# Hand-ordered instruction lists for a two-layer conditional block: new first and last lists, the condition joined to self outside TensorE, q/k halves spread over three engines

## The chip, the cores and the metric

One core of one Trainium2 chip. The metric is the device time of one launch in microseconds (us). The engines are TensorE (PE, with its weight loads PEld), VectorE (DVE), ScalarE (ACT) and GpSimd (POOL); SyncE (SP) issues every DMA of this kernel.

## The reference, cut to what matters

Eight batches of 256 tokens and 256 features go through two layers, in float32. Layer 0 is a graph attention, layer 1 a transformer block whose norms are set by a condition vector of the batch.

```
# layer 0, F = 256, 16 heads, 20 keys
q_exp = where(v.sum(-1) == 0, 0, q[:, None, :])          # the condition, dropped for all-zero rows
self_feat = concat([v, q_exp]) @ W_self.T + b_self
for d in range(2):                                       # two directions of the adjacency
    cond = A_d.sum(-1); vb = A_d @ w_bias + b_bias
    aff = where(cond > 0, qh @ kh / 4, NEG) + vb         # qh, kh from self_feat
    output += (softmax(aff) @ kv) @ Wout_d + bout_d
x = v + relu(output)
# layer 1, 16 heads of 16, S = 256
nx = ada_rmsnorm(x, cond, ...)
q, k, v = nx @ wq + bq, nx @ wk + bk, nx @ wv + bv       # q and k rotated (rope)
x = x + softmax(q @ k / 4) @ v @ wo + bo
nx = ada_rmsnorm(x, cond, ...)
x = x + (gelu(nx @ w_gate) * (nx @ w_up)) @ w_down       # 1024 hidden
```

## The kernel before

**Numbers in two halves.** The large products run on operands split in a rounded high half and the rest, the low half. `product` (L1076 on) makes three matmuls of each: high by high, high by low, low by high. So each activation and each weight passes two steps: a high half (a copy that rounds), and a low half (whole minus high). For weights these are `whigh` on ACT and `wlow` on POOL or DVE, one per piece of 512 columns, 19 pieces; pieces are loaded by DMA into 11 slots, and a slot is loaded again only once `wlow` of its first piece is done. Six of the slots lie in the tile `ya`, which also holds the condition's weights, the rotated q/k (`t1`, `t2`), their halves and the exponentials.

**Stages of one batch.** Layer 0: x^T is loaded; `xh`, `xl` split it; `rsum` multiplies it by ones, for each token's row sum; `nz` (L789) makes of it 1 or 0, times a one-hot column of the batch; `selfm` (L1134) makes the self product, and its last matmul (L1145) adds the condition: `qz`, which holds the high and low parts of the condition's product for all batches, by `nzT`. `selfc` (ACT, L528) adds the bias and writes `self32`; `selfh` (DVE, L820) and `selfl` (POOL) split it. `kv0`, `kT`, `q0` give keys, values and queries; `affm` the affinities in two halves c; then for each half `am` (DVE, mask), `aadd` (POOL, L387, mask offset), `amax` (DVE), `asub` (POOL), `aexp` (ACT), `asums` (DVE), `aprob` (POOL), transposes `pTt` with copies `pTv`, `pTa`. `y`, `yadd`, `x1T`, `x1add` end layer 0. Layer 1: a norm (`square1`, `rms1`, `xr_scaled`, `nxT`, `nxc`, `nxh`, `nxl`), `qk`, `v`; `rot` (DVE, L912) makes the two terms of the rotation and `radd` (POOL, L438) adds them, for both token halves; `qkT` transposes q (n = 0) and k (n = 1); `qkadd` (DVE, L927) adds the bias and then makes the high half, `qklow` (POOL, L444) the low one. Both n use the one tile `qk32`, so `qkadd(1)` waits for `qklow(0)`. The halves go to HBM and come back stacked (`store_hi`, `store_lo`, `stack`: 9 DMAs). `s(0)` to `s(15)` are score products for the row maxima (`mx`), `nmT`, `nrowc`, `nrows` put the maxima next to the queries, `st(0)` to `st(15)` make the shifted scores, `exph` exponentiates them, `pv`, `oc`, `oT`, `onorm`, `aT`, `ah`, `al`, `wo` end the attention; `x2add`, a second norm (to `nzl`), then `gate`, `up`, `down` with `gelu`, `hmul`, `hh`, `hlow`, and `result`.

**Condition.** `cond_q` gives the self layer's share of the condition, one row per batch, `qparts` (DVE, L745) splits it; `cond_1`, `hidden_cond`, `cond_2` (32 matmul records at L1111) and `table` (DVE, L774) give the scales and shifts of both norms.

**Order.** Nothing is scheduled at run time. Each engine has a list written out by hand, `round_` (L313 SP, L464 POOL, L662 ACT, L1002 DVE, L1392 PE), called by `rounds` (L228) for `it` = -3 to 9. A round works on up to four batches at once: layer 0 of batch it+1, the middle of batch it, the attention of it-1 and its end and the feed-forward part of it-2. `step` (L218) leaves a step out where its batch does not exist; `once` (L223) places the steps that occur once (loads, weight halves, constants) somewhere in the same list. So the first and the last batches keep the order of the middle ones. Engines run their lists in order and wait on semaphores.

## Time and profile before

| | us |
|---|---|
| median of 3 runs | 568.94 (567.25 to 571.3) |
| the profiled execution | 569.02 |
| its span, first to last instruction | 567.4 |

Outside the span lie 1.6 us. Times in rows are us from the start of the span. The stores of the eight results are issued at 199.8, 256.9, 314.0, 371.1, 428.1, 478.4, 524.8 and 564.8. In rows, L1081 is `product`, L1118 `transposes` and L377 `low`, helpers of many steps: the tile names tell which. A float32 matmul counts as two records, one of a split product as one.

### The profile page before, as it was taken

To read this page: it belongs to the slowest core of one execution; us is meant where nothing else is said; L and a number is where in the kernel's file an instruction comes from. 1 tells how busy PE (TensorE), PEld (TensorE's weight loads), DVE (VectorE), ACT (ScalarE), POOL (GpSimd) and SP (SyncE) were. 2 spreads that over 40 slices of the span, in tenths; PEclk is the share of its full clock that TensorE was granted. 3 is DMA by queue.
4 is the path that set the end of the run, shared out by engine and by line. 5 is a ranking of instruction groups with operands and counts; after the bars stand their busy time and mean duration, and the time that the engine had idled before them with its cause. 6 is when DMAs were issued, how large, how long until landed. Compare 5 with 4: busy or idle time off the path is not lost. (4 is left out here: it accounts for less than half of the span.)

```text
span 567.4 us, 9625 instructions
## 1 busy us (share of the span) xinstructions
PE 468.3 (83%) x3644; PEld 397.0 (70%) x3644; DVE 325.0 (57%) x597; ACT 237.7 (42%) x465; POOL 231.2 (41%) x203
## 2 busy tenths in 40 slices
PE   0387773878799979998999899989998898699567
PEld 0266462756599858985898589858986796498366
DVE  0835676585685667566856686667664753461111
ACT  3115221125444553555355545454555346227222
POOL 0735167228324822482348233823382253211022
PEclk9996695599999999999999999999999999889879
DMA  8812202502801080109010901090009003600000
GB/s 281 301 43 74 88 1 92 94 2 72 186 1 63 10 205 2 57 16 204 2 49 25 204 1 41 32 205 1 22 2 203 1 3 120 86 1 3 20 0 20
DMA packets 33276, 40.22 MB, mean 71 GB/s; under 512 B 3152, under 2 KB 28240, under 8 KB 32976
## 3 DMA queue, kind: packets, MB, share of 16 engines
q1 hardware_dynamic: 33232, 39.61, 27.1%
q8 instruction: 30, 0.49, 0.4%
q14 instruction: 14, 0.11, 0.1%
HBM read 28.85 MB, written 10.49 MB: 69 GB/s over the span
## 5 line engine op out<-in xcount | busy, mean ns | idle before, releaser
L1081 PE MATMUL ps<-splz,wh 128*128 128x256 f32 x512 | 98.9, 288 | 3.0 <-POOL splz L377 3.0
L942 DVE TENSOR_REDUCE nm<-ps 128x2 f32<-128x512 f32 x128 | 84.5, 688 | 17.8 <-PE ps L1277 16.7
L603 ACT ACTIVATE ya<-ps 128x512 f32<-128x512 f32 x128 | 72.0, 599 | 52.6 <-PE ps L1301 51.1
L377 POOL TENSOR_TENSOR hs<-g,hs 128x512 fp32r<-128x512 f32 x32 | 41.4, 1293 | 107.1 <-ACT hs L659 107.1
L1081 PEld LDWEIGHTS ps<-splz,wh 128*128 128x128 f32 x512 | 80.7, 194 | 5.5 <-issue 5.4
L1081 PE MATMUL ps<-splz,wl 128*128 128x256 f32 x256 | 72.9, 285 | 0.0
L1277 PE MATMUL ps<-kst,qst 96*128 96x256 f32 x256 | 52.8, 306 | 6.2 <-DVE nm L942 3.0
L1081 PE MATMUL ps<-wh,hs 128*128 128x256 f32 x256 | 55.8, 285 | 0.8 <-POOL hs L377 0.8
L1301 PE MATMUL ps<-qst,kst 100*128 100x256 f32 x256 | 53.5, 306 | 2.4 <-ACT ya L603 1.5
L649 ACT ACTIVATE g<-ps 128x512 f32<-128x512 f32 x32 | 19.2, 600 | 72.8 <-PE ps L1081 72.8
L1081 PEld LDWEIGHTS ps<-splz,wl 128*128 128x128 f32 x256 | 49.4, 193 | 0.0
L1301 PEld LDWEIGHTS ps<-qst,kst 100*128 100x128 f32 x256 | 37.9, 189 | 15.5 <-ACT ya L603 13.2
L1277 PEld LDWEIGHTS ps<-kst,qst 96*128 96x128 f32 x256 | 39.6, 198 | 10.9 <-DVE nm L942 7.4
L1081 PEld LDWEIGHTS ps<-wh,hs 128*128 128x128 f32 x256 | 43.3, 188 | 1.0 <-POOL hs L377 1.0
L1081 PE MATMUL ps<-splx,wh 128*128 128x256 f32 x192 | 40.5, 306 | 1.7 <-DVE x L894 1.2
L993 DVE TENSOR_TENSOR g<-ps,g 128x512 f32<-128x512 f32 x32 | 22.0, 688 | 31.9 <-PE ps L1081 31.3
L1316 PE MATMUL ps<-ya,vv 128*32 128x256 f32 x512 | 34.3, 385 | 6.0 <-ACT ya L603 6.0
L1081 PE MATMUL ps<-wh,sply 128*128 128x256 f32 (+1 forms) x128 | 38.2, 359 | 0.0
L1081 PE MATMUL ps<-wl,hs 128*128 128x256 f32 x128 | 35.8, 279 | 0.0
L1081 PEld LDWEIGHTS ps<-splx,wh 128*128 128x128 f32 x192 | 32.4, 208 | 3.9 <-issue 3.0
L412 POOL TENSOR_TENSOR prob<-aff,arc 128x640 f32<-128x640 f32 x16 | 20.4, 1274 | 34.9 <-PE ps L1201 26.6
L1201 PE MATMUL ps<-const_sb,prob 128*128 128x128 f32 x128 | 23.2, 317 | 8.9 <-POOL prob L412 8.9
(136 smaller groups left out, 970.7 us busy)
## 6 DMA issues: line engine op xcount, KB each, us to landing
qk_d<-ya SPq DMA_DIRECT2D x16, 512.0 KB, 2.8
qst<-qk_d SPq DMA_DIRECT2D x24, 256.0 KB, 5.1
kst<-qk_d SPq DMA_DIRECT2D x48, 128.0 KB, 5.9
adjD<-adj SPq DMA_DIRECT2D x8, 440.0 KB, 4.1
ya<-wall SPq DMA_DIRECT2D x12, 256.0 KB, 4.5
xT<-xt SPq DMA_DIRECT2D x8, 256.0 KB, 2.7
x_add<-x SPq DMA_DIRECT2D x8, 256.0 KB, 3.7
result<-xr SPq DMA_DIRECT2D x8, 256.0 KB, 3.1
```

The lines of the kernel that those rows point to most:

```text
L377: pool.tensor_tensor(into, whole, high.bitcast(FP32), ALU.subtract).then_inc(signal.sem, 1)
L412: pool.tensor_tensor(prob[:, :, 0:M], aff[:, c].rearrange("p d h m -> p (d h) m"), arc[:, c, :].unsqueeze(2).broadcast_to([P, 2 * H, M]), ...
L603: act.activation(ex[:, h % EXR], ps[:, h % 2].rearrange("p (c s) -> p c s", c=TC), ACT.Exp, scale=SCALE).then_inc(ex_ok.sem, 1)
L649: act.activation(g32[:, j % 2], ps[:, BANK["g"]].rearrange("p (k s) -> p k s", k=2), ACT.Gelu).then_inc(gelu_ok.sem, 1)
L942: dve.tensor_reduce(nm[:, :, h], ps[:, h % 2].rearrange("p (c s) -> p c s", c=TC), AX.X, ALU.max, negate=True).then_inc(mx_ok.sem, 1)
L993: dve.tensor_tensor(g, ps[:, BANK["u"]].rearrange("p (k s) -> p k s", k=2), g, ALU.mult).then_inc(hm_ok.sem, 1)
L1081: ins = pe.matmul(dst, lhs(a, k), rhs(c, k), start=first_ and n == 0 and m == 0, stop=last_ and n == len(ks) - 1 and m == 2, **kw)
L1201: ins = pe.transpose(ps[:, BANK["pT"][d], g * P:(g + 1) * P], prob[:, at:at + 4, :].rearrange("p h m -> p (h m)"), ident)
L1277: ins = pe.matmul(ps[:, h % 2, c * S:(c + 1) * S], qst[0:96, h // 2, c * P:(c + 1) * P], kst[0:96, h, :], start=True, stop=True)
L1301: ins = pe.matmul(ps[:, h % 2, c * S:(c + 1) * S], kst[0:100, h, c * P:(c + 1) * P], qst[0:100, h // 2, :], start=True, stop=True)
L1316: ins = pe.matmul(ps[32 * j:32 * j + 32, BANK["o"], (g % 2) * S:(g % 2 + 1) * S], vv[b % 2][:, c, h, :], ex[:, h % EXR, c, :], start=c == ...
```

## The change

1. **Lists.** `program(head, round_, tail)` replaces `rounds`: a head list of each engine written out for the first batches, `round_` for it = 2 to 6, a tail list for the last ones. Loads and once-only steps stand in the head in the order of first use. In `round_` some steps change place: `pTt(0)` from the end of a round to the next one, between `st(15)` and `pv(3)`; `rsum` ahead of `x1T`; `kv0`, `q0`, `st(0)` with other neighbours; `aprob(1)`, `x1bias`, `rms2`, `nzl`, `hlow` at other ends of POOL's list; the result's store ahead of `store_lo`.
2. **Condition and self.** `cond_q` gives columns instead of rows (8 matmul records of 8 columns instead of 4 of 256); `qcols` (DVE) copies them. `nz` has no one-hot any more; `qb` (ACT) makes `qbias = nz * qcol + b_self`; the matmul L1145 goes (2 per batch), and `selfadd` (DVE) writes `self32` from PSUM plus `qbias`. `selfc` goes; `selfh` moves from DVE to ACT.
3. **q/k.** `radd(1)` moves to DVE (`radd1`); `qkadd` only adds, the high halves are made on ACT (`qkhigh`), the low half of q on POOL (`qlow`), that of k on DVE (`klow`). k has a tile of its own (`k32`), so `qkadd(1)` waits for nothing but its transposes.
4. **`aadd`** moves from POOL to DVE.
5. `cond_2` and `table` are split by layer (`n` = 0, 1), the last 1 MB of the condition's weights is a load of its own (`wc3`).

```diff
-        def rounds(round_):
-            for it in range(-3, B + 2):
-                round_(it)
+        def program(head, round_, tail):
+            head()
+            for it in range(2, 7):
+                round_(it)
+            tail()
...
-            def selfc(b):
-                act.wait_ge(self_ps.sem, self_ps.at(b))
...
+            def qb(b):
+                act.wait_ge(nz_ok.sem, nz_ok.at(b))
...
+                for k in range(KC):
+                    ins = act.activation(qbias[:, k, :], nzT[:], ident_fn, scale=qcol[:, k, b:b + 1], bias=vec[:, V_BSELF + k:V_BSELF + k + 1])
+                ins.then_inc(qb_ok.sem, 1)
+            def selfh(b):
+                act.wait_ge(self_ok.sem, self_ok.at(b))
+                act.activation(splx[:, 0], self32[:], ACT.Copy).then_inc(selfh_ok.sem, 1)
...
+            def selfadd(b):
+                dve.wait_ge(self_ps.sem, self_ps.at(b))
+                dve.wait_ge(qb_ok.sem, qb_ok.at(b))
+                dve.tensor_tensor(self32[:], ps[:, BANK["self"]].rearrange("p (k s) -> p k s", k=KC), qbias[:], ALU.add).then_inc(self_ok.sem, 1)
...
-                    pe.matmul(ps[:, BANK["self"], o * S:(o + 1) * S], qz[:, o * P:(o + 1) * P], nzT[:], start=False, stop=True).then_inc(self_ps.sem, 1)
...
+            def radd1(b):
+                dve.wait_ge(rot_ok.sem, rot_ok.at(b))
+                dve.tensor_tensor(t1[:, 1], t1[:, 1], t2[:, 1], ALU.add).then_inc(radd1_ok.sem, 1)
...
-                    if n:
-                        dve.wait_ge(qkl_ok.sem, qkl_ok.at(b, n))
...
-                    dve.wait_ge(qk_ok.sem, qk_ok.at(b, n + 1))
-                    dve.tensor_copy(qkh[:, 2 * n:2 * n + 2].bitcast(F32R), qk32).then_inc(qkh_ok.sem, 1)
...
+            def qkhigh(n):
+                def step(b):
+                    act.wait_ge(qk_ok.sem, qk_ok.at(b, n + 1))
+                    act.activation(qkh[:, 2 * n:2 * n + 2].bitcast(F32R), qk32[n], ACT.Copy).then_inc(qkh_ok.sem, 1)
...
+            def klow(b):
+                dve.wait_ge(qkh_ok.sem, qkh_ok.at(b))
+                dve.wait_ge(qkT_ps.sem, qkT_ps.at(b))
+                dve.tensor_tensor(qkl[:, KC:2 * KC].bitcast(F32R), qk32[1], qkh[:, KC:2 * KC], ALU.subtract).then_inc(kl_ok.sem, 1)
```

The new lists, each in its order, several steps to a line here; the number in the last bracket is the batch, in `round_` relative to `it`.

```
SP head   load_xt(0), qk 1, rope, self 0, cond, vec, wb, load_adj(0), wkv, angles, q0 0, q0 1, g 0, consts,
          qk 0, g 2, wc2, u 3, g 1, g 3, bo, load_xt(1), u 1, u 2, load_adj(1), u 0, o 0, v 0, wc3,
          load_x_add(0), d 1, d 2, ...
DVE head  nz(0), zeros(1), zeros(0), wlow self, qcols, adjm(0), selfadd(0), wlow q0 x2, vb, kbadd, bout, mask, kb (0),
          rotated_bias, wlow qk x2, am0, aadd0, amax0, am1, aadd1, amax1, asums0 (0), ones(0), asums1, pTv0 (0),
          ones(1), pTv1(0), adjm(1), yadd(0), nz(1), x1add(0), table(0), xr_scaled(0), selfadd(1), wlow v, nxh(0),
          vb, kbadd (1), rot0, rot1, radd1 (0), kb, mask (1), qkadd0, qkadd1, klow (0), ... mx(0)(0) ...
PE head   rsum(0), cond_q, selfm x2 (0), kv0, q0(0,1), kT, q0 x3, affm0, affm1 (0), cond_1, pTt0, pTt1 (0),
          cond_2(0), pTt2, pTt3 (0), cond_2(1), y, x1T (0), rsum, selfm x2 (1), nxT(0), kv0, kT (1), qk x2 (0), ...
ACT round exph(7), xh(+1), exph(8), exph(9), qkhigh(0)(-1), qkhigh(1)(-1), oc(0), exph(10) to exph(13), aexp(1)(0),
          exph(14), exph(15), oc(1) (-2), ...
DVE round ... hmul(3)(-2), am(1), amax(0) (+1), rot0, rot1, radd1 (0), aadd(1), asums(0) (+1), qkadd0, qkadd1 (0),
          amax(1)(+1), result(-2), klow(0)
PE round  st(12), st(13), pv(2), st(14), st(15) (-2), pTt(0)(0), pv(3)(-2), pTt(1)(0), oT0, oT1 (-2), pTt(2)(0),
          aT(-2), v(1)(-1), pTt(3)(0), wo x2 (-2), y(0), rsum(+1), x1T(0), v(0), s(0) (-1), nzTr(-2), ...
```

## Rows read from the trace of the kernel before

**Rows 1.** The page: busy us, granted clock and DMA rate in 40 slices

```profile
PE 468.3 (83%) x3644; PEld 397.0 (70%) x3644; DVE 325.0 (57%) x597; ACT 237.7 (42%) x465; POOL 231.2 (41%) x203
PEclk9996695599999999999999999999999999889879
...
GB/s 281 301 43 74 88 1 92 94 2 72 186 1 63 10 205 2 57 16 204 2 49 25 204 1 41 32 205 1 22 2 203 1 3 120 86 1 3 20 0 20
```

**Rows 2.** Stretches: length, busy us of PE, PEld, DVE, ACT, POOL; clock, DMA, GB/s

```profile
0.00:141.47 141.47, 87.45 (x505) 68.96 (x505) 82.65 (x144) 40.83 (x82) 63.19 (x57) 0.83 0.34 105
...
312.71:369.80 57.09, 53.71 (x451) 46.21 (x450) 37.80 (x71) 27.98 (x56) 26.75 (x24) 1.00 0.28 69
...
426.88:477.01 50.13, 45.14 (x372) 38.16 (x371) 27.94 (x53) 24.30 (x48) 17.20 (x17) 1.00 0.27 60
477.01:524.10 47.09, 39.35 (x316) 34.27 (x315) 18.07 (x36) 20.67 (x39) 9.46 (x9) 0.93 0.30 63
524.10:567.40 43.30, 27.86 (x212) 24.61 (x210) 8.03 (x16) 12.03 (x24) 7.30 (x7) 0.88 0.04 13
```

**Rows 3.** Order of time, PE: first gate, q transposed, pv(3), x1T

```profile
390.27 0.40 PE L1081 MATMUL ps<-splz,wh 128*128 128x256 f32 x2
...
421.61 0.60 PE L1118 MATMUL ps<-const_sb,ya 128*128 128x128 f32 x4
...
430.35 1.07 PE L1316 MATMUL ps<-ya,vv 128*32 128x256 f32 x16 [0.69 <-ACT ya L603]
...
441.53 0.63 PE L1118 MATMUL ps<-const_sb,l 128*128 128x128 f32 x4 [1.07 <-DVE l L884]
```

**Rows 4.** Groups by line and shape in one round, 312.71 to 369.80

```profile
L390 POOL TENSOR_TENSOR aff<-aff,off 128x640 f32<-128x640 f32 x2 | 3.1, 1567 | 0.2 <-DVE aff L854 0.2
L854 DVE TENSOR_TENSOR aff<-ps,msk 128x640 f32<-128x640 f32 x2 | 1.6, 818 | 1.4 <-PE ps L1184 1.4
L448 POOL TENSOR_TENSOR ya<-ya 128x512 fp32r<-128x512 f32 x3 | 3.9, 1290 | 1.9 <-DVE ya L936 1.9
L933 DVE TENSOR_TENSOR ya<-ps,rbT 128x512 f32<-128x512 f32 x2 | 1.4, 692 | 2.8 <-POOL ya L448 1.5 <-PE ps L1118 1.3
L936 DVE CAST ya<-ya 128x512 fp32r<-128x512 f32 x2 | 1.1, 554 | 0.1
L805 DVE TENSOR_REDUCE cw<-adjD 128x80 f32<-128x880 int32 x1 | 1.1, 1062 | 0.0
L1145 PE MATMUL ps<-nzT,qz 128*128 128x256 f32 x2 | 0.6, 277 | 0.0
L526 ACT ACTIVATE splx<-xT 128x512 fp32r<-128x512 f32 x1 | 0.6, 622 | 0.0
```

**Rows 5.** Tile wl: duration min/median/max in ns, of DVE's weight halves

```profile
L770 DVE TENSOR_TENSOR wl<-ya,wh x10: 620/1019/1754, 15.6 to 83.5; 128x512 fp32r<-128x512 f32 x10
```

**Rows 6.** Order of time, first batch: start us, us, engine line

```profile
8.32 0.45 SPq L253 DMA_DIRECT2D xT<-xt  x1
...
17.31 1.76 DVE L734 MEMSET kst<- 96x2048 f32 x1 [0.37 <-issue]
...
18.91 4.96 POOL L377 TENSOR_TENSOR splx<-xT,splx 128x512 fp32r<-128x512 f32 x1
...
23.92 1.22 PE L1130 MATMUL ps<-splx,onesr 128*128 128x256 f32 x4 [5.84 <-POOL splx L377]
...
29.86 0.84 ACT L535 ACTIVATE self<-ps,vec 128x256 f32<-128x256 f32 x2 [13.26 <-PE ps L1145]
...
65.00 0.69 DVE L894 SCALAR_TENSOR_TENSOR x<-ps,x_add 128x512 f32<-128x512 f32 x1
...
109.98 0.96 PE L1277 MATMUL ps<-kst,qst 96*128 96x256 f32 x4
...
129.31 0.71 PE L1301 MATMUL ps<-qst,kst 100*128 100x256 f32 x4 [0.36 <-issue]
```

**Rows 7.** Order of time, the last batch's first scores

```profile
491.68 0.47 PE L1277 MATMUL ps<-kst,qst 96*128 96x256 f32 x2 [2.37 <-DMA kst<-qk_d]
```

More of the change, by code:

```diff
@@ new lines, in round_, with tail @@
+            def round_(it):
+                step(load_adj, it + 2)
+                store_hi(it)
+                store(it - 2)
+                store_lo(it)
+                stack(it)
+                nrows(it)
+                step(load_x_add, it + 2)
+                step(load_xt, it + 3)
+            def tail():
+                store_hi(7)
+                store(5)
+                store_lo(7)
+                stack(7)
+                nrows(7)
+                store(6)
+                store(7)
@@ L352, in _ @@
+            program(head, round_, tail)
             sp.wait_ge(res_out.sem, 16 * B)
@@ new lines, in tail @@
+            def tail():
+                nxl(7)
+                hlow(3)(5)
+                radd0(7)
+                qlow(7)
+                x1bias(7)
+                rms2(6)
+                nzl(6)
+                hlow(0)(6)
+                hlow(1)(6)
+                hlow(2)(6)
+                hlow(3)(6)
+                rms2(7)
+                nzl(7)
+                hlow(0)(7)
+                hlow(1)(7)
+                hlow(2)(7)
+                hlow(3)(7)
+            program(head, round_, tail)
@@ L727, in _ @@
+            program(head, round_, tail)
         @block.vector
@@ L1075, in _ @@
+            program(head, round_, tail)
         @block.tensor
@@ L1102, in cond_1, with cond_2, step @@
                             ins = pe.matmul(ps[:, 1, (2 * n + o) * B:(2 * n + o + 1) * B], wc[:, at:at + P], cT[:, k, :], start=k == 0, stop=k == KC - 1)
[L1103 to L1107 removed]
+                ins.then_inc(c1_ps.sem, 1)
+            def cond_2(n):
+                def step():
+                    if n:
+                        pe.wait_ge(wc3_in.sem, wc3_in.at(0))
+                    pe.wait_ge(h_ok.sem, h_ok.at(0))
                     for o in range(4):
@@ L1491 @@
+            program(head, round_, tail)
 _IN = ["xt", "x", "adj", "condT", "wall", "wsmall", "wcond", "cols", "rows_in", "tabs", "consts"]
```

1380 lines of the change are left out of this document (997 added, 383 removed).

## The prediction

> **What bounds the kernel now.** I read the shares of busy time first, then busy time in stretches cut at the moments at which a batch's result is added, then the order of time inside one such stretch, and last the order of time of the first batch. The shares name PE (83%), but as an average over stages [rows 1]. The stretches part the span in three [rows 2]. A full round takes 57.08 us five times over, 141.47 to 426.88: PE is busy 53.7 of it, DVE 37.8, ACT 28.0, POOL 26.8. In it PE is the bound, with little left. Before it lie 141.5 us in which PE is busy 87 at a mean granted clock of 0.83; the clock row shows 5 or 6 tenths in four of the first eight slices, the 1.2 GHz level for part of each [rows 1]. After it lie 140.6 us (50.1, 47.1 and 43.3) with the work thinning out. So half of the time is head and tail, ordered by a list made for the middle: there is the room.
>
> The rounds first. A float32r matmul of 256 columns follows the last one after about 0.118 us (the six of a product take 0.7); the work of a round summed at such paces comes to some 51.5 us, so about 5.5 are waits. They sit in one place: from pv(3) at 430.35, which waited for the last exponential, to the next round's first gate product at 390.27 + 57.08 = 447.35, lies a serial chain of 17.0 us (output transposes, normalisation, wo, second norm), in which PE runs only what fills it [rows 3]. From the gate to the end of q's transposes (421.61 + 0.60) it is 31.9 us and PE is nearly full; from there to pv(3), 8.1 us, with 6.6 us of work in it and 1.5 of waits for exponentials [rows 3].
>
> **The rounds, edit by edit.** *Condition out of TensorE:* two matmuls less, 2 x 0.118 = 0.24 us of PE per batch (277 ns each from start to end, of which most overlaps) [rows 4]. Its replacement (`qb` and `selfadd`, about 0.8 on ACT in place of `selfc`, 0.69 on DVE) hides beside the score products. *q/k halves:* today the chain on DVE and POOL is add 0.69, cast 0.55, POOL subtract 1.29, and again the same, since one tile serves both: the second add waits 1.5 us for the subtract [rows 4]. Afterwards both adds run back to back. But what they free is the store and the stacking, and in a round `s(0)` is found ready; so nothing on the path, except that `radd1` on DVE (0.69 for POOL's 1.29) lets `qkT` start earlier. *`aadd`:* 1.57 on POOL becomes 0.82 (the like of L854) on DVE, twice: the softmax of layer 0 is 1.5 us shorter, off the path. On DVE the sum is 2 x 0.82 + 3 x 0.69 added, 0.43 + 2 x 0.55 removed, some +2.2 of 37.8; on ACT two high halves of q/k and one of self, 3 x 0.62, of 28.0 [rows 2, 4]. Both engines idle a third of the round.
>
> *Order:* `rsum` fills part of the 1.07 us at `x1T` [rows 3], but that lies inside the 17.0 us chain, which no filler shortens: it counts nothing. The chain keeps its length (each of its steps stays behind the same step on DVE, the adjacency sums of 3 x 1.06 included [rows 4]). `pTt(0)` moves into the wait before pv(3): 0.55 us hidden. Two down products stand between `st(11)` and `st(12)` instead of one, so the exponentials catch up: from q's transposes to pv(3) I count 6.2 us of PE work and 0.5 of wait, 6.7 for 8.1. From gate to `qkT(0)`: the work is 30.7 (two `st` more, two matmuls less); `st(0)` comes after fillers, so its 0.5 us wait goes; I get 31.0 to 31.7 for 31.9, and take 31.3. Sum 17.0 + 31.3 + 6.7 = **55.0 us**.
>
> *What the moved work may cost.* ACT's list now has `qkhigh(0)` and `(1)` ahead of exp 10 to 15, so six exponentials wait for DVE's two adds, which queue behind `aadd(1)` and `asums(0)`. If DVE is in time this costs nothing; bounds 0 and, from DVE's idle time, some 15 us. And DVE subtracts or adds from SBUF alone take 0.62 us or up to 1.75 [rows 5], the long ones while POOL runs. Four such per round (2 `aadd`, `radd1`, `klow`) cost DVE 0 to 4 us more, of which only `radd1` and the `aadd` before it stand near the path. I take 0.4: **55.4 us per round**, bounds 54 (the gate chain and PE's work alone) and 59.
>
> On this the Trainium skill has a rule (SBUF — State Buffer, Who interferes with whom): a VectorE instruction with two SBUF inputs contends with a GpSimd instruction that reads SBUF, and the later one blocks entirely. The trace agrees in the spread of rows 5. By it the four moved operations speak against this change; what it gives at its worst is a rival below.
>
> **The head.** Milestones of batch 0 now: row sums at 23.9, self ready at 30.7, x1 at 65.7, `s(0)` at 110.0, `st(0)` at 129.3, end of head 141.5 [rows 2, 6].
> *To self.* xT was the fifteenth DMA, at 8.3; then POOL's `xl` took 4.96 us. Now xT goes first and lands at about 3.5, 0.62 and 1.27 us of halves, row sums at 5.6. But DVE's list has `nz`, then the two kst memsets (2 x 1.76), then the self weights' low half, so the self product starts at 11.3, and `selfadd` stands behind the adjacency sums (3.2): self at 15.2, **15.5 earlier**.
> *To x1.* Today 35.0. The same chain, but SP holds `u 3` and all behind it until DVE has made the low half of `qk 0`, at about 25; ACT waits for `g 1` to some 29 with the first `aexp` behind it; one more table load (1.3); and all of `cond_2` stands before `y` and needs the 1 MB load at the end of 40 pieces' worth of bytes, which at the 281 to 301 GB/s of the first slices [rows 1] is about 40. I get x1 at 51, 36 us after self: no gain here, a loss of 1.
> *To s(0).* Today 44.3. DVE's list holds about 25 us of work there (rotation, three weight halves, batch 1's layer 0), and the q/k chain with its stack needs about 27. `s(0)` at **78**.
> *To st(0).* Today 19.3. Now batch 1's and 2's layer-0 steps lie between the maxima: DVE has 16 x 0.69 plus 8 us, then 5 for the row of maxima through DMA: 25.5, `st(0)` at 103.5.
> *To the end.* As today, 12: head ends at **115.5**. Check from below: DVE was busy 82.7 us in the head [rows 2]; the change adds 6 `aadd`, 2 `radd1`, 2 `klow`, 3 `selfadd` and takes 3 self and 4 q/k casts, +6.8, so 89.5 after its first instruction at 6: no head is shorter than 96. Bounds 98 and 128.
>
> **The tail.** 50.1 becomes 48.1 by the round's gains; in the next stretch `s(0)` of batch 7 waited 2.37 us for the stack [rows 7], which comes about 0.5 sooner, but the gate waits for the norm chain anyway: 1 us for denser filling. The last 43.3 is one batch's chain, untouched. 137.5 for 140.6, bounds 135 and 141.
>
> **Sum**, against the profiled execution (span 567.4, 569.0 in all, 0.1 above the median of 568.9): 115.5 + 5 x 55.4 + 137.5 + 1.6 outside = **531.6**, say 531.5.
>
> **Rivals.**
> A (forecast): 531.5, own range 523 to 540. Chance 0.48.
> B: only the head gains; PE's rounds stay at 57.1 because the chain and the exponentials wait in new places. For it: PE's busy share hardly falls. Against: 1.4 us of waits have a visible filler. 115.5 + 285.4 + 140.6 + 1.6 = 543. Chance 0.19.
> C: the head gains half, since DVE is its bound and the loads were not: SP's block at `u 3` or the memsets push everything. Head 128.5: 544.5. Chance 0.12.
> D: better than I count: head 105, rounds 54, tail 136: 512.5. Chance 0.12.
> E: the rule on the ports at its worst: all four operations blocked and on the path, rounds 59, head 121.5: 121.5 + 295 + 138 + 1.6 = 556; with some more of the same in the head it reaches 563. Chance 0.06.
> F: slower than before. The exponentials queued behind `qkhigh` on ACT wait d us in every round for DVE's adds; with them st(12) to pv(3) and the whole chain to the gate. Five rounds and one of the tail: 531.5 + 6d. For it: ACT runs in order and DVE is 4 to 6 us fuller. Against: DVE idles 19 us of the round. It decides from d = 7.2, where it passes 574.6; at d = 8, 579.5. Chance 0.03.
> That the lists don't do what they say would need the head's first products no earlier than 20 us; xT is plainly first, so this has no chance of its own.
>
> **How the numbers follow.** Likeliest is A: 531.5. The range 512 to 550 holds A, B, C and most of D, 0.85 and more of the chance. Slower or faster by under 1%, about what a measurement of this kernel can tell, is 563 to 575: only the upper half of E, 0.03. Slower is F, 0.03; faster all else, 0.94.
>
> **What would show it.** Right: first matmul near 6 us, x1 of batch 0 near 51, `s(0)` near 78, first full round starting near 115, results 55.4 apart, PE busy 53 in each with the granted clock of the head above 0.83; no wait of ACT's exponentials on `qk32`'s adds above 1 us. Wrong: results 57 apart (B); DVE idle under 5% of a head of 128 (C); the moved adds at 1.5 us and `qkT` waiting for `radd1` (E); exp(10) idle on DVE's add for several us (F); DVE waits in the head under 5 us with a head of 105 (D).

## The result, and the profile after

The median went from 568.1 to 550.9 us (four runs each, 566.8 to 571.3 and 548.8 to 551.3); the ratio is 0.968, 95% interval 0.963 to 0.973. That is 17 us for 37 forecast, and 0.9 us outside the range. The profiled execution after took 551.3 us with a span of 549.5. "Faster" came true, the size did not.

The busy shares and the clock row of the page after, against [rows 1]:

```profile
PE 468.5 (85%) x3632; PEld 404.1 (74%) x3632; DVE 341.3 (62%) x612; ACT 250.4 (46%) x489; POOL 186.8 (34%) x170
...
PEclk9955787999999999999999999999999999699779
```

Busy time in stretches, cut as in [rows 2] where a batch's result is added (columns: stretch, length, busy us of each engine, granted clock, DMA share, GB/s): the head, a full round, and the last three stretches.

```profile
0.00:126.30 126.30, 88.92 (x500) 73.58 (x501) 86.48 (x149) 46.13 (x92) 47.77 (x45) 0.82 0.39 114
182.37:238.41 56.04, 52.92 (x449) 46.20 (x448) 40.23 (x72) 29.43 (x58) 21.41 (x20) 1.00 0.32 71
406.41:456.46 50.05, 45.56 (x376) 38.81 (x374) 29.37 (x53) 25.24 (x50) 15.26 (x15) 1.00 0.29 59
456.46:505.65 49.19, 41.50 (x316) 35.93 (x315) 18.44 (x36) 20.93 (x39) 8.57 (x8) 0.90 0.28 58
505.65:549.50 43.85, 27.99 (x212) 24.98 (x210) 8.03 (x16) 11.40 (x22) 7.29 (x7) 0.84 0.04 13
```

| part | before | forecast | after | miss |
|---|---|---|---|---|
| head | 141.5 | 115.5 | 126.3 | +10.8 |
| five rounds | 285.4 | 277.0 | 280.1 | +3.1 |
| tail | 140.6 | 137.5 | 143.1 | +5.6 |

(A round is 56.04 us, the fifth 55.9.) So the head gave most of what there was, each round 1.04 us, and the tail became 2.5 us longer.

The first batch in order of time after, which answers to [rows 6] (start us, us, engine line):

```profile
5.34 1.22 PE L1545 MATMUL ps<-splx,onesr 128*128 128x256 f32 x4 [5.34 <-POOL splx L409]
...
12.00 0.55 PE L1491 MATMUL ps<-splx,wh 128*128 128x256 f32 x1 [3.71 <-DVE wl L992]
...
14.94 0.69 DVE L1043 TENSOR_TENSOR self<-ps,qbias 128x512 f32<-128x512 f32 x1
...
53.72 0.68 DVE L1122 SCALAR_TENSOR_TENSOR x<-ps,x_add 128x512 f32<-128x512 f32 x1
...
69.42 0.69 DVE L1166 TENSOR_TENSOR ya<-ps,rbT 128x512 f32<-128x512 f32 x1
...
74.81 0.34 SPq L288 DMA_DIRECT2D qst<-qk_d  x1
...
88.61 0.75 PE L1689 MATMUL ps<-kst,qst 96*128 96x256 f32 x4 [2.81 <-DMA kst<-qk_d]
...
113.28 0.71 PE L1713 MATMUL ps<-qst,kst 100*128 100x256 f32 x4 [0.52 <-issue]
```

Step by step, forecast and measured: to self 15.2 and 14.9; to x1(0) 35.8 and 38.8; to s(0)(0) 27 and **34.9**; to st(0)(0) 25.5 and 24.7; to the end of the head 12 and 13.0. (These are counted from the starts of the rows. The forecast counted from the ends of self and x1, 0.7 later, which makes the third step 34.2.) Most of the head's miss is one step, and its row ends in a wait for the stack's transfer.

A round, which answers to [rows 3]: pv(3), the first gate, q's transposes, the next pv(3).

```profile
353.55 1.07 PE L1728 MATMUL ps<-ya,vv 128*32 128x256 f32 x16 [0.50 <-ACT ya L687]
...
370.54 0.41 PE L1491 MATMUL ps<-splz,wh 128*128 128x256 f32 x2
...
402.01 1.04 PE L1533 MATMUL ps<-const_sb,ya 128*128 128x128 f32 x8
...
409.58 1.07 PE L1728 MATMUL ps<-ya,vv 128*32 128x256 f32 x16 [0.50 <-ACT ya L687]
```

From pv(3) to the gate it is 16.99 us, as forecast (17.0). From the gate to the end of q's first transposes (402.01 + 0.60) 32.07, where 31.3 stood. From there to pv(3) 6.97, for 6.7. The moved operations in one round, groups by shape, against [rows 4]:

```profile
L1173 DVE TENSOR_TENSOR ya<-k,ya 128x512 fp32r<-128x512 f32 x1 | 1.7, 1661 | 0.0
L1082 DVE TENSOR_TENSOR aff<-aff,off 128x640 f32<-128x640 f32 x2 | 1.6, 816 | 0.0
L1157 DVE TENSOR_TENSOR ya<-ya 128x512 f32<-128x512 f32 x1 | 0.7, 691 | 0.0
L660 ACT ACTIVATE ya<-ya 128x512 fp32r<-128x512 f32 x1 | 0.6, 622 | 0.0
```

`aadd` and `radd1` run at their undisturbed pace and `qkhigh` on ACT waits for nothing (idle before: 0.0). `klow` alone is slow, 1.66 us. Rival E, which needs all four slow and on the path, and rival F are out by these rows.

### The profile page after: what moved, and what is told of

It reads as the page before. It is cut to its first block and busy times, and to the rows that moved or that the text cites. A ratio compares the mean times of both kernels' runs of the same rounds, so it can differ in the third digit from the quotient of the medians.

```text
span 549.5 us, 9618 instructions
## 1 busy us (share of the span) xinstructions
PE 468.5 (85%) x3632; PEld 404.1 (74%) x3632; DVE 341.3 (62%) x612; ACT 250.4 (46%) x489; POOL 186.8 (34%) x170
## 5 line engine op out<-in xcount | busy, mean ns | idle before, releaser
L1491 PE MATMUL ps<-splz,wh 128*128 128x256 f32 x512 | 101.1, 293 | 3.0 <-POOL splz L409 3.0
L1491 PEld LDWEIGHTS ps<-splz,wh 128*128 128x128 f32 x512 | 82.8, 199 | 5.8 <-issue 5.7
L1491 PE MATMUL ps<-splz,wl 128*128 128x256 f32 x256 | 74.1, 290 | 0.0
L1689 PE MATMUL ps<-kst,qst 96*128 96x256 f32 x256 | 54.1, 312 | 9.2 <-DMA kst<-qk_d 6.0
L1491 PE MATMUL ps<-wh,hs 128*128 128x256 f32 x256 | 54.3, 284 | 1.0 <-POOL hs L409 1.0
L1713 PE MATMUL ps<-qst,kst 100*128 100x256 f32 x256 | 49.5, 303 | 2.9 <-ACT ya L687 2.1
L1491 PEld LDWEIGHTS ps<-splz,wl 128*128 128x128 f32 x256 | 50.8, 198 | 0.0
L1491 PE MATMUL ps<-wh,sply 128*128 128x256 f32 (+1 forms) x128 | 39.9, 371 | 0.3 <-issue 0.3
L1491 PEld LDWEIGHTS ps<-splx,wh 128*128 128x128 f32 x192 | 33.1, 212 | 8.7 <-issue 8.0
```

The costliest lines, as they stand in the source:

```text
L1491: ins = pe.matmul(dst, lhs(a, k), rhs(c, k), start=first_ and n == 0 and m == 0, stop=last_ and n == len(ks) - 1 and m == 2, **kw)
L1689: ins = pe.matmul(ps[:, h % 2, c * S:(c + 1) * S], qst[0:96, h // 2, c * P:(c + 1) * P], kst[0:96, h, :], start=True, stop=True)
L1713: ins = pe.matmul(ps[:, h % 2, c * S:(c + 1) * S], kst[0:100, h, c * P:(c + 1) * P], qst[0:100, h // 2, :], start=True, stop=True)
```

## The experiments

Each row of the table is one run: medians and ratios against the kernel before on the same chip; head (the first result less the gap to the second), mean round and tail (from the fifth result on) from its profiled execution. A head or a tail repeats less well than a round. Three kernels with the very same head (the change, tail_fill, tail_round) differ by 0.5 us in it; six with the very same tail (the change, head_fill, stack_free, loads_early, zeros_later, mx_first) by 2.8, 143.1 to 145.9. The kernel before was timed again beside each group of runs, at 568.1 to 570.9, so small differences between two runs are better read from the ratios than from the medians.

| run | median | ratio, interval | head | round | tail |
|---|---|---|---|---|---|
| the change | 550.9 | 0.968 (0.963-0.973) | 126.3 | 56.0 | 143.1 |
| lists_only | 585.5 | 1.029 (1.023-1.034) | 149.2 | 59.1 | 142.6 |
| rev_self | 562.8 | 0.987 (0.983-0.990) | 137.2 | 55.8 | 143.6 |
| rev_qk | 562.3 | 0.984 (0.979-0.989) | 130.7 | 56.8 | 147.3 |
| rev_aadd | 560.7 | 0.984 (0.979-0.989) | 132.0 | 57.6 | 143.3 |
| self_consts | 552.3 | 0.969 (0.963-0.975) | 127.7 | 55.8 | 142.2 |
| tail_round | 559.4 | 0.982 (0.979-0.985) | 126.4 | 56.1 | 150.5 |
| tail_fill | 547.5 | 0.961 (0.955-0.966) | 125.9 | 56.0 | 138.3 |
| head_fill | 546.7 | 0.960 (0.956-0.964) | 123.3 | 56.0 | 145.9 |
| stack_free | 554.7 | 0.974 (0.970-0.978) | 127.9 | 56.0 | 143.3 |
| loads_early | 549.6 | 0.965 (0.962-0.968) | 124.7 | 56.0 | 143.7 |
| zeros_later | 551.5 | 0.967 (0.963-0.970) | 127.8 | 56.0 | 143.3 |
| mx_first | 561.8 | 0.985 (0.982-0.988) | 134.5 | 56.0 | 145.7 |
| combo1 | 544.8 | 0.955 (0.951-0.959) | 123.8 | 56.0 | 139.6 |
| combo2 | 543.8 | 0.954 (0.952-0.957) | 122.9 | 56.0 | 138.5 |
| combo3 | 545.4 | 0.958 (0.956-0.960) | 125.3 | 55.8 | 138.2 |
| combo4 | 541.2 | 0.951 (0.946-0.956) | 119.2 | 56.0 | 140.2 |

### What the lists do, and what the moved operations do

**lists_only** keeps all new lists and puts the three groups of operations back into their old form and onto their old engines.

```diff
-                radd1(0)       # DVE
-                klow(0)
+                radd1(0)       # POOL; klow, aadd(0), aadd(1) too
-                qkhigh(0)(0)   # ACT
+                dve.tensor_copy(qkh[:, 2 * n:2 * n + 2].bitcast(F32R), qk32[n]).then_inc(qkh_ok.sem, 1)
```

> The new order of loads and lists, but the operations of the kernel before in their old form: condition in TensorE's self product, both q/k halves' casts on DVE in one tile, radd1, the k low half and aadd on POOL. Theory 1 (order does nearly all; the moved operations change only engines with room, and a round is bound by PE's own work): rounds 56.0 to 56.8, head 126 to 130, the whole 551 to 558. Theory 2 (the moved operations eat the gain through the shared ports, rival E in a mild form): without them the rounds fall to 55.4 or less and the whole to 543 to 548. Theory 3 (the moved operations carry the gain): rounds back at 57 and the head at 133 or more, 560 to 567.

Measured: 585.5 us, slower than the kernel before, outside all three theories. Its rows (one in the head, then one round in order of time, PE and DVE):

```profile
16.16 0.48 DVE L1030 TENSOR_SCALAR nzT<-ps,const_sb 128x256 fp32r<-128x256 f32 x1 [16.16 <-DMA const_sb<-consts]
...
255.70 0.82 DVE L1096 TENSOR_REDUCE amx<-aff 128x32 f32<-128x640 f32 x1 [2.14 <-POOL aff L423]
...
262.01 1.06 PE L1517 MATMUL ps<-const_sb,ya 128*128 128x128 f32 x8 [1.37 <-POOL ya L482]
...
265.29 0.69 DVE L1171 TENSOR_TENSOR ya<-ps,rbT 128x512 f32<-128x512 f32 x1 [1.46 <-POOL ya L478]
```

Here is what I had costed at nothing. In the new lists each step follows closely on the last: DVE's next instruction stands right behind the one that hands over to POOL. With the additions on POOL, DVE waits 2.14 for a maximum's input and 1.46 for a q/k tile, PE 1.37 for the rotation; and DVE's first instruction waits 16.2 us for the constants, which the new order loads fourteenth. With the operations in their old form, and at the places in POOL's list where I put them (I tried no others), the new lists lose against the old ones. The next three runs put the groups back one at a time.

**rev_self:** `qb`, `selfadd` and `qcols` back to two matmuls in the self product and the old `nz`, which reads the constants.

```diff
+                dve.wait_ge(consts_arr.sem, consts_arr.at(0))
+                dve.tensor_scalar(nzT[:], ps[:, BANK["rs"], 0:S], 0.0, hot[:, b:b + 1], ALU.not_equal, ALU.mult).then_inc(nz_ok.sem, 1)
```

> The changed kernel with one operation group back in its old form: the condition joins the self product in TensorE, with the old row normalisation, which reads the constants. The run with all three groups back (585.5, against 550.9) had its first self product at 23.0 instead of 12.0, because DVE's first instruction waited for the constants, fourteenth in the new order of loads, and rounds of 58.9. Theory 1 (this group is a condition of the early start, not a saving of matmuls): the first self product at 23, the head 8 to 10 us longer, rounds 56.2 to 56.4 (two matmuls more), 559 to 563 in all. Theory 2 (the delay of self is absorbed, since weights and loads set x1): head +3 or less, 553 to 556.

Measured: 562.8; the head 10.9 us longer, rounds 0.2 us *shorter*. Theory 1 for the head and the total, but not for its longer rounds. (The first self product comes at 21.0, in lists_only at 21.6; the 23.0 of the expectation is the condition's matmul behind it.)

**rev_qk:** one q/k tile, both casts on DVE, `radd1` and `klow` on POOL. (POOL's `qlow(1)` stands ahead of `asub(1)(2)`, since DVE's second addition needs it.)

```diff
-                radd1(it)      # DVE
-                klow(it)
+                radd1(it)      # POOL
+                klow(it)
```

> The changed kernel with the q/k halves back in their old form: one tile, both casts on DVE, the second half's addition and k's low half on POOL. Theory 1 (POOL's list in the new order puts work of the next batch's layer 0 ahead of the addition for which q's transposes wait): q's transposes wait 1 us or more for POOL, DVE waits 1.5 for POOL's q low half, a round takes 57 to 58, head +3 to +5, 559 to 567 in all. Theory 2 (the two engines have room, as my forecast said: nothing on the path but radd1): rounds 56.0 to 56.6, head +2, 552 to 556.

Measured: 562.3; rounds 56.8, just under theory 1's 57, head +4.4, tail +4.2. The round's extra 0.7 lies between q's transposes and pv(3): 7.69 for 7.0. Theory 1 is half right: DVE waits 1.46 for POOL's low half of q, but the transposes come as before (32.06 from the gate for 32.07). Of the tail's 4.2, 2.9 lie in its first stretch, 52.9 us at a granted clock of 0.94 where the change has 50.05 at 1.00; what of them is the clock and what the edit no run parts.

**rev_aadd:** `aadd(0)` and `aadd(1)` on POOL, around `asub(0)`.

```diff
+                aadd(0)(it + 1)
                 asub(0)(it + 1)
+                aadd(1)(it + 1)
```

> The changed kernel with the two softmax additions of layer 0 back on POOL. Theory 1 (DVE's list stands right behind them, so each round trip DVE to POOL to DVE stalls the chain that ends at q's transposes): DVE waits 1 to 2 us at each maximum, a round takes 57 to 58, 556 to 562 in all. Theory 2 (off the path, as my forecast said): rounds within 0.3 of 56.0, the head +1 at most, 551 to 553. Theory 3 (a port gain: DVE no longer meets POOL): rounds 55.5, 547 to 550.

Measured: 560.7, theory 1; the round's 1.5 us lie between the gate and q's transposes (33.6 for 32.07), and the maximum waits for POOL as in lists_only:

```profile
294.80 0.82 DVE L1097 TENSOR_REDUCE amx<-aff 128x32 f32<-128x640 f32 x1 [2.13 <-POOL aff L422]
```

By the medians the three singles cost 11.9, 11.4 and 9.8, together 33.1, and all at once 34.6. By the ratios it is 5.0% together and 6.0% at once, and a round loses 2.2 us by the singles and 3.1 at once: they add only roughly.

**self_consts:** rev_self with one load moved.

```diff
                 load_xt(0)
+                get_consts()
                 weights("qk", 1)()
...
-                get_consts()
```

> The condition's join in its old form (two matmuls in the self product), as in the run that took 562.8 us with a head 10.7 us longer and rounds of 55.83, but with the constants loaded second instead of fourteenth. Theory 1 (only the place of that load held the start): the first self product at 12.5 to 14, the head within 2 us of the changed kernel's, rounds 55.83 again, 549 to 552 in all. Theory 2 (the old form's additional steps on DVE and ACT cost the head something themselves): the head 3 to 6 us longer, 553 to 556.

Measured: 552.3; the first self product at 12.3, head +1.4, rounds 55.8. Theory 1, a little over its interval: 9.5 of the 10.9 us were the place of the constants, not TensorE's two matmuls. So of this group it is the independence from the constants that the new lists need.

### The tail

**tail_round:** the tail's own lists are left out and the round's run on, each entry guarded by its batch number.

```diff
-            for it in range(2, 7):
+            for it in range(2, B + 2):
                 round_(it)
-            tail()
```

> The changed kernel without its own lists for the last batches: the round's lists run on to the end, each operation guarded by its batch number. Theory 1 (the tail list gives little; its 143.1 us against 140.6 before are clock and chains): last three stretches 50.0 + 47.5 to 49.5 + 43 to 44, 550 to 552. Theory 2 (the tail's own list is what the change gains there, and without it the tail would be worse): the last three 3 to 6 us longer, 554 to 557. Theory 3 (the tail list is what lost the 2.6 us): 141 or less, 548 to 549.

Measured: 559.4, beyond theory 2: the tail takes 150.5 for 143.1. The new round's order is worse for the last batches than the old one (140.6), and the tail's own lists earn 7.4 us, which only nearly makes up for it.

**tail_fill:** matmuls into a PSUM bank that nobody reads any more (`fill(n, bank)` repeats one product of the self weights with themselves).

```diff
+                fill(22, 4)
                 s(0)(7)
...
+                fill(27, 4)
                 nzTr(7)
+                fill(22, 4)
                 gate(0, 0)(7)
```

> The changed kernel plus matmuls in the tail whose result nobody reads (22 ahead of s(0)(7), then 5, 14, 27 and 22 ahead of the last batch's output transposes, wo, second-norm transposes and gates), placed where PE only waits. Theory 1 (the 5.6 us that the tail lacks against the forecast are mostly matmuls at the 1.2 GHz level after idle stretches): the granted clock stays at 1.00 from 468 on, the gates of batch 6 take 0.12 and not 0.21 each, the last stretch's 64 matmuls take 8 instead of 10.1, and the kernel is 3 to 5 us faster than the changed one (546 to 548). Theory 2 (the gates wait for other engines anyway, or the fillers delay their followers): clock up, time within 1 us of 551. Theory 3 (the clock does not answer to such matmuls): clock 0.90 and 0.84 as before and nothing gained or 1 us lost.

Measured: 547.5, tail 138.3. Stretches of 4 and 6 us about the gates of the last two batches; first the changed kernel:

```profile
468.00:472.00 4.00, 0.83 (x5) 0.56 (x5) 1.44 (x4) 0.91 (x4) 2.16 (x3) 0.95 0.40 58
...
476.00:480.00 4.00, 3.96 (x19) 3.93 (x19) 1.22 (x2) 1.88 (x2) 0.00 (x0) 0.50 0.00 0
...
524.00:530.00 6.00, 4.80 (x24) 4.83 (x25) 0.00 (x0) 1.88 (x2) 1.06 (x1) 0.53 0.00 0
```

and with the fillers:

```profile
468.00:472.00 4.00, 3.32 (x27) 2.97 (x26) 1.47 (x4) 0.91 (x4) 2.19 (x3) 1.00 0.20 24
...
476.00:480.00 4.00, 4.00 (x29) 4.00 (x28) 1.29 (x2) 1.11 (x2) 0.00 (x0) 0.77 0.02 4
...
519.00:525.00 6.00, 5.61 (x47) 5.43 (x46) 0.43 (x1) 2.88 (x4) 1.28 (x1) 1.00 0.00 0
```

Without them PE is busy 0.83 of 4 us, waiting for the last batch's stack, and then runs its full 4 us at 0.50, the 1.2 GHz level: 19 matmuls where 29 fit at 0.77. The clock answers to work that nobody needs. It did not stay at 1.00 throughout, as theory 1 had it: it still dropped for a part of 472 to 480. The gain is 4.8 us of tail in the profiled executions and 3.4 by the medians, whose ratios (0.961 and 0.968) have intervals that overlap. That it is real shows in the table: five kernels with these fillers have tails of 138.2 to 140.2, the six with the tail as it was 143.1 to 145.9. The Trainium skill has the rule (TensorE: Matmul & The Clock Gate, Why this matters for your kernels): gaps in TensorE's work between bursts of matmuls bring its rate down, so avoid them. These two runs agree, 0.50 against 0.77 from 476 to 480 us and 143.1 against 138.3 us of tail.

### The head

**head_fill:** the same, ahead of five entries of the first batch's layer 0.

```diff
+                fill(16, 2)
                 q0(0, 1)(0)
...
+                fill(11, 2)
                 cond_1()
+                fill(32, 2)
                 pTt(0)(0)
```

> The changed kernel plus unread matmuls in the first batch's layer 0: 16 ahead of q0(0,1), 6 and 5 ahead of the two affinity products, 11 ahead of cond_1, 32 ahead of pTt(0). In the changed kernel PE runs at the 1.2 GHz level from about 28 to 66 us, with 17 us of condition products, transposes and y in a row on the way to x1(0). Theory 1 (this stretch is bound by PE at half clock): the granted clock stays at 1.00 until 50, x1(0) comes at 46 to 49 instead of 53.7, half or more of it is left at the end of the head, and the whole is 2 to 6 us faster (545 to 549). Theory 2 (the 1 MB condition load, or DVE, sets x1): clock up, x1 within 1 us, time 550 to 552. Theory 3 (fillers only push the queue): x1 later by 1 to 3, 552 to 554.

Measured: 546.7. One stretch of the changed kernel, then of this one:

```profile
28.00:66.00 38.00, 30.98 (x142) 26.27 (x143) 20.93 (x35) 13.67 (x27) 19.12 (x15) 0.55 0.36 123
```

```profile
28.00:66.00 38.00, 32.63 (x206) 27.42 (x207) 24.60 (x43) 13.67 (x27) 19.93 (x15) 0.78 0.41 134
```

The granted clock rises from 0.55 to 0.78, x1(0) comes at 50.3 for 53.7, and 3.0 us are left at the end of the head: theory 1, though the clock did not stay at 1.00 and x1(0) came later than its 46 to 49. (The profiled execution is the slowest of five, 551.2; the others took 546.1 to 546.9. Its head counts here, its tail does not.)

**stack_free:** `load_x_add(1)` and `weights("d", 0)` behind the first stack.

```diff
-                load_x_add(1)
-                weights("d", 0)()
                 store_lo(0)
                 stack(0)
+                load_x_add(1)
+                weights("d", 0)()
```

> The changed kernel with load_x_add(1) and the d 0 weight piece (0.5 MB) issued behind the first batch's low store and stack instead of ahead of them. Theory 1 (the stack's transfers of batch 0, 7.7 us at the median and 9.7 the last, share the DMA engines with these two): s(0)(0) at 85 to 86 instead of 88.6, and 1 to 3 us off the whole (548 to 550). Theory 2 (the stack is slow by itself, 128 partitions in small packets): s(0)(0) comes earlier only by the 1.3 us of SP's issue, 550 to 551. Theory 3 (DVE's list sets the maxima, whatever the stack does): s(0)(0) earlier and the end of the head unchanged, 551.

Measured: 554.7, slower than any theory. s(0)(0) came 3.9 us earlier, but nobody was there to use it:

```profile
84.73 0.74 PE L1689 MATMUL ps<-kst,qst 96*128 96x256 f32 x4 [0.41 <-DMA kst<-qk_d]
...
88.19 0.82 DVE L1095 TENSOR_REDUCE asum<-aff 128x32 f32<-128x640 f32 x1 [4.65 <-ACT aff L628]
...
89.31 1.22 DVE L1178 TENSOR_REDUCE nm<-ps 128x2 f32<-128x512 f32 x2
```

ACT's list has the high half of `d 0` ahead of batch 1's exponentials; the later load held ACT for 7.5 us, ACT held DVE, and DVE's first maximum came at 89.31 (89.15 in the changed kernel).

**loads_early:** both loads to where their buffers are already free.

```diff
                 load_x_add(0)
+                weights("d", 0)()
                 weights("d", 1)()
...
+                load_x_add(1)
                 store_hi(0)
-                load_x_add(1)
-                weights("d", 0)()
```

> The changed kernel with load_x_add(1) and the d 0 piece issued where their buffers are already free (before d 1, and before the first high store) instead of between the high and the low store. In an earlier run they went behind the stack: s(0)(0) came at 84.7 instead of 88.6, but the first maximum still at 89.3, because DVE then waited 4.6 us for an exponential that stood on ACT behind the late d 0 piece. Theory 1 (the transfers share the DMA engines, and this time nothing else moves): s(0)(0) at 85 to 86, the first maximum at 86 to 87, the end of the head 1 to 2.5 us earlier, 548.5 to 550 in all. Theory 2 (from the first maximum on DVE's and PE's lists of batch 1 set the pace): the end of the head unchanged, 550.5 to 551.5.

Measured: 549.6, theory 1; s(0)(0) at 84.3, first maximum at 85.4. The transfers issued about the stack (KB each, median us to landing), changed kernel first, then this one:

```profile
kst<-qk_d SPq DMA_DIRECT2D x6, 128.0 KB, 7.7
```

```profile
kst<-qk_d SPq DMA_DIRECT2D x6, 128.0 KB, 5.6
```

In a round, with little beside them, the same transfers land after 5.2. Of 4.3 us at s(0)(0), 1.6 are left at the end of the head. (The median is 1.3 us lower, with intervals that overlap; it is the profile that shows the effect.)

**zeros_later:** the two memsets of the key stack behind `pTv(1)(0)`.

```diff
-                zeros(1)()
-                zeros(0)()
...
                 pTv(1)(0)
+                zeros(1)()
+                zeros(0)()
```

> The changed kernel with DVE's two memsets of the key stack (1.76 us each, second and third in its list) behind the last transposed probability of batch 0, in an idle stretch of DVE. Theory 1 (the start chain is DVE's, as my forecast of self had it): the first self product at 9 instead of 12.0, selfadd at 11.7 to 12.5, but x1(0) no more than 1 us earlier because condition loads and PE at half clock set it: 550 to 551. Theory 2 (DVE's start carries through to x1): x1(0) at 50.5 to 51, 547.5 to 549. Theory 3: a longer idle stretch of PE lowers the clock earlier and gives it back, 551 to 552.

Measured: 551.5. The first self product comes at 8.6, but `selfadd` only at 14.1, since DVE now waits 2.2 us for the adjacency load. x1(0) comes 1.4 us earlier and x1 of batch 1 1.2, yet the head ends 1.5 later. The loss lies between x1 of batch 1 and its q addition, where the same 147 matmuls met another granted clock; the changed kernel first, then this one:

```profile
98.06:122.63 24.57, 20.30 (x147) 15.85 (x146) 19.96 (x38) 10.87 (x25) 8.05 (x8) 1.00 0.04 13
```

```profile
96.86:124.08 27.22, 23.02 (x147) 18.44 (x146) 20.16 (x38) 11.00 (x25) 8.07 (x8) 0.87 0.04 11
```

So the memsets held the start, and the clock took back more than their move gave. Theory 3 had a lower clock, but an earlier stretch for it.

**combo1** is tail_fill and head_fill together, with `cond_2(1)` behind `x1T(0)`.

```diff
-                cond_2(1)()
                 y(0)
                 x1T(0)
+                cond_2(1)()
```

> Unread matmuls in the head and in the tail together (546.7 and 547.5 each by itself, 550.9 without), and the second half of the condition product moved from ahead of y(0) to behind x1T(0). Theory 1 (PE at half clock held x1(0), and the second condition half stood ahead of y without need): x1(0) at 47 to 49, head 3 to 6 us shorter than the 126.3 of the changed kernel, last two stretches 47.4 + 37.5, 539 to 543 in all. Theory 2 (the head is bound behind x1 by DVE's list): x1 early, st(0)(0) at 110 as with the head's fillers alone, 542 to 544. Theory 3: the moved condition product delays nxT(0) and the move gains nothing or loses 1 to 2.

Measured: 544.8, above the intervals of both theories (539 to 543 and 542 to 544). s(0)(0) is 1.8 us earlier than with the head's fillers alone, st(0)(0) 0.6 later: the move gains nothing, as theory 3 had it. Even the 1.8 can't be credited to it: 1.5 of them lie between x1 and q's addition, 14.15 us at a granted clock of 0.81, and tail_round has the same 14.16 at 0.81 without the move.

**mx_first** asks what then sets the end of the head: the sixteen maxima of batch 0 in a row, the steps of batches 1 and 2 behind them.

```diff
                 s(3)(0)
-                y(1)
                 s(4)(0)
...
                 s(15)(0)
+                y(1)
+                rsum(2)
+                x1T(1)
                 nmT(0)
```

> The changed kernel with all sixteen score maxima of batch 0 in a row, and y(1), x1 of batch 1 and the self product of batch 2 behind them instead of between them; row copy and first exponentials moved up on ACT. Theory 1 (the head ends with batch 0's own chain): first maximum to st(0)(0) 14 to 18 us instead of 24.1, and the first result 3 to 6 us earlier, 545 to 548 in all. Theory 2 (batches 1 and 2 have to be fed by the end of the head anyway, so DVE and PE work is conserved): st(0)(0) 6 to 10 us earlier, the first result within 1.5 us of 182.4, 550 to 552. Theory 3 (the maxima alternate with their score products over two banks and leave both engines half idle): the first result 2 to 5 us later, 553 to 556.

Measured: 561.8, beyond theory 3. In order of time:

```profile
92.18 1.29 DVE L1178 TENSOR_REDUCE nm<-ps 128x2 f32<-128x512 f32 x2 [0.29 <-PE ps L1689]
...
93.76 1.29 DVE L1178 TENSOR_REDUCE nm<-ps 128x2 f32<-128x512 f32 x2 [0.29 <-PE ps L1689]
```

A pair of maxima takes 1.58 us (93.76 - 92.18), all sixteen 13 us. But x1 of batch 1 slipped from 98.1 to 107.1, the first result from 182.4 to 190.5, and st(0)(0) by only 1.5. The place of `nmT` behind y(1) was mine and cost batch 0 its gain, so theory 1 had no clean trial. On who sets the end it does say something. From the first q/k addition of batch 1 to the first result it is 59.7 us in the changed kernel and 59.5 to 60.1 in thirteen other runs, this one among them (59.6): all that were made but rev_qk, rev_aadd and lists_only, which change that part itself. From st(0)(0) to the first result it is just as steady in the others (68.9 to 69.4), so they can't tell the two chains apart; here they part, 75.7 from st(0)(0) and 59.6 from batch 1's addition. In this one run the end follows batch 1.

**combo2** is combo1 without the condition's move, with loads_early and 60 more fillers ahead of s(0)(0).

```diff
+                fill(12, 2)
                 affm(0)(1)
...
+                fill(20, 2)
                 pTt(0)(1)
...
+                fill(14, 2)
                 s(0)(0)
```

> Unread matmuls in head and tail as before, 60 more of them in the head between 66 and 88 us (12, 8, 6, 20 and 14 ahead of the two affinity products of batch 1, v(1)(0), pTt(0)(1) and s(0)(0)), and the two transfers issued early. Theory 1 (clock and transfers add up): x1(0) at 50.3, s(0)(0) at 80 to 82, head 121 to 122.5, tail as in the tail run (47.4 + 37.3), 541 to 543. Theory 2 (behind s(0)(0) the head is set by DVE's list of maxima and batch 1): the head at 123.4 as with the first fillers alone, 543 to 545. Theory 3 (fillers ahead of pTt and s delay them): 545 to 547.

Measured: 543.8, in theory 2's interval in the total and between 1 and 2 in the head (122.9). From 66 to 92 us the granted clock is now 1.00, where it was 0.82:

```profile
66.00:92.00 26.00, 18.80 (x148) 17.01 (x146) 22.46 (x37) 9.89 (x19) 13.20 (x10) 1.00 0.46 102
```

and s(0)(0) still comes at 82.9, as in combo1. But from x1 to q's addition (50.7 to 66.4, below) it still ran at 0.74.

**combo3** is combo2 with self_consts.

```diff
                 load_xt(0)
+                get_consts()
```

> The run with all unread matmuls and early transfers (543.8 us) with the condition's join in its old form and the constants loaded second. Theory 1 (its parts add up): rounds 55.83 instead of 56.04, the head no longer than 1 us more, 542 to 544. Theory 2 (the self start comes later and nothing behind absorbs it): the head 2 to 5 us longer, 545 to 548.

Measured: 545.4, theory 2: five rounds give 1.1 us, the head takes 2.4 back.

**combo4** is combo2 with fillers in that stretch too.

```diff
+                fill(6, 2)
                 y(0)
+                fill(14, 2)
                 x1T(0)
...
+                fill(9, 2)
                 selfm(1)(1)
...
+                fill(9, 2)
                 kT(1)
```

> combo2 with 50 more unread matmuls between the second condition half and q's transposes of batch 0 (6, 6, 14, 9, 9 and 6 ahead of cond_2(1), y(0), x1T(0), selfm(1)(1), kT(1) and qkT(0)(0)). Theory 1 (the clock is part of what the step x1(0) to s(0)(0) lost): granted clock 1.00 from 44 to 66, x1(0) 1 to 2 us earlier than 50.7, x1 to q's addition 12.5 to 14 us instead of 15.7, the head 1.5 to 3 us shorter than 122.9, 541 to 542.5. Theory 2 (handovers between DVE, ACT, POOL and PE bind it): clock up, the step still 15 us or more, the head within 1 us, 543 to 544.5. Theory 3 (fillers stand in the way of work that is ready): 545 or more.

Measured: 541.2, theory 1 and beyond it in the head (119.2). First combo2 from its x1 to q's addition, then combo4 from 44 to 66:

```profile
50.70:66.40 15.70, 12.42 (x67) 9.88 (x68) 9.15 (x25) 3.43 (x9) 4.68 (x5) 0.74 0.35 113
```

```profile
44.00:66.00 22.00, 19.44 (x149) 16.91 (x147) 14.81 (x37) 7.67 (x18) 7.22 (x7) 1.00 0.45 147
```

x1(0) comes at 46.8, q's addition 13.6 us later instead of 15.7, s(0)(0) at 78.4. Of these 4.5 us 3.6 stay at the end of the head. The clock is not yet at its upper level throughout: from x1 of batch 1 to its q addition this kernel takes 27.8 us at 0.82, where the change took 24.6 at 1.00. This is the fastest version of the study: 4.9% under the kernel before, where the change is 3.2% under it. (No run compares the two directly.)

## Why the prediction was right or wrong

**The head, 10.8 of the missing 20 us.** The step that failed is "the q/k chain with its stack needs about 27. `s(0)` at 78". It took 34.9 from the start of x1 (34.2 from its end, from which the forecast counts): 15.7 from x1 to q's addition, 5.4 to the stack's issue, 13.8 to s(0)(0). About 3 of the excess is the stack landing beside 0.5 MB of other transfers (loads_early: 13.8 becomes 11.0), for which the 27 had no term. About 2 are the clock: x1 to q's addition takes 15.7 at a granted clock of 0.74, 13.6 at full clock (combo4), and 14.2 at 0.81 in tail_round, whose head is the changed kernel's own:

```profile
53.72:69.42 15.70, 12.41 (x67) 9.85 (x68) 9.16 (x25) 3.43 (x9) 4.69 (x5) 0.74 0.30 97
```

```profile
53.73:67.89 14.16, 11.12 (x67) 8.83 (x68) 9.17 (x25) 3.43 (x9) 4.70 (x5) 0.81 0.35 108
```

combo4 shows the chain without either hindrance. Its stack is issued from 65.4 on, the DMA engines have nothing left from 75.1 on (first row: their busy tenths from 65 to 80 us, in 40 slices), and the last transfer is signalled at 75.6. s(0)(0) comes later because transposes and 14 unread matmuls of mine stand ahead of it:

```profile
DMA  9998799998999999999999995210000000000000
...
76.37 2.20 PE L1539 MATMUL ps<-wh 128*128 128x256 f32 x14
78.41 0.64 PE L1693 MATMUL ps<-kst,qst 96*128 96x256 f32 x4
```

Its chain is 13.6 + 5.0 + 10.2 = 28.8 us, 28.1 from the end of x1. Against 27 that leaves about 1 of the 7 us too many, for which the cause stays open. The second failure is "I get x1 at 51", 53.7 measured: the sum had no term for PE's pace there, and 28 to 66 us ran at 0.55; at full clock x1 is at 46.8. The 25.5 and the 12 behind s(0)(0) held to 1 us, but in part by luck: I followed batch 0, and in the one run that parts the two it is batch 1's chain that sets the end (mx_first).

**The tail, 5.6.** "50.1 becomes 48.1 by the round's gains" failed: 50.05. Two of its three parts did gain (to the gate 19.5 for 20.4, behind q's transposes 3.8 for 4.3), but from the gate to the end of q's transposes it takes 26.7 for 25.4, with PE busy nearly all the time in both; before first, then after:

```profile
447.30:472.72 25.42, 25.42 (x208) 23.79 (x207) 14.36 (x27) 12.15 (x20) 10.04 (x9) 1.00 0.01 3
```

```profile
425.92:452.65 26.73, 26.30 (x212) 24.51 (x211) 15.85 (x28) 14.60 (x27) 8.65 (x8) 1.00 0.01 3
```

So the new list brings PE slightly more work there (212 matmul records for 208), where the forecast had it bring less; which steps these are I have not taken apart. And "1 us for denser filling" met the other clock level: the gates of the last two batches ran at half clock, which costs the 3.4 to 4.8 us of tail_fill. I had both rows of the clock before me and gave them no term.

**The rounds, 3.1.** The chain of 17.0 held: 16.97 to 17.03 in 50 of 54 full rounds (three of every kernel, the one before included), and at most 17.16 (self_consts). The mis-sized term is "from gate to qkT(0): the work is 30.7". PE is busy for all of it:

```profile
314.49:346.00 31.51, 31.51 (x264) 29.46 (x263) 22.06 (x42) 16.75 (x33) 11.64 (x10) 1.00 0.10 33
```

My sum of work at bare column paces was less than PE is busy; [rows 2] had it, busy 53.7 where I summed 51.5. What fills the difference no run takes apart. The second term, 6.7, measured 6.97. That the q/k halves put "nothing on the path" and that `aadd` is "off the path" was wrong: under these lists they are worth 0.7 and 1.5 us a round (rev_qk, rev_aadd), because DVE then no longer waits for POOL.

**The rivals.** B (543) had the rounds unchanged and the head as forecast. C (544.5) was nearest in kind, but the memsets are no cause of the size it gave (zeros_later) and DVE idles nearly a third of the head; SP's block at `u 3` was not tested. D is refuted by the head of 126.3, F by the rows above. E: the moved operations meet POOL in two ways. `klow` starts at 182.97, 0.17 us after a subtraction of POOL (`xl` of a later batch), and takes 1.66 us; at 407.02, where POOL runs nothing beside it, it takes 0.68. `aadd` starts at 168.96, 0.16 us ahead of a subtraction of POOL (`nxl`), and keeps its 0.82; there POOL takes 1.79 where it takes 1.27 at 60.2. The Trainium skill (SBUF — State Buffer, Who interferes with whom) has it that the order of issue decides who is blocked, and the trace agrees. But `klow` stands behind the result and ends before pv(3), off the path, and the 0.4 us taken for such delays are not seen in the chain.

## What to carry to other kernels

Time a chain at the head or tail of a kernel from the granted clock of that very stretch, and when PE has a gap there of which the next work is on the path, filling it with unread matmuls is cheap: it gave 3 us in the head (7 with more of it and two earlier transfers) and 3 to 5 in the tail. Count them a little under the gap: in combo4 14 of them stood ahead of a product whose operands had landed. Lists written out in strict order and the placement of operations on engines are one decision: the same lists were 3% slower than before with the old placement. In a pipelined head ask which batch's chain sets the end before shortening the first one's. And before crediting an edit with a microsecond or two of the head, look at the granted clock of the stretches that it did not touch.
